# Row maxima of attention scores from sums and differences of two key halves, with two heads stacked on the contraction rows

## The reference

```python
q = (hn @ wq + bq).reshape(b, s, NH, D).transpose(0, 2, 1, 3)
k = (hn @ wk + bk).reshape(b, s, NH, D).transpose(0, 2, 1, 3)
v = (hn @ wv + bv).reshape(b, s, NH, D).transpose(0, 2, 1, 3)
scores = jnp.einsum('bhqd,bhkd->bhqk', q, k) / jnp.sqrt(jnp.float32(D))
attn = jax.nn.softmax(scores, axis=-1)
o = jnp.einsum('bhqk,bhkd->bhqd', attn, v)
```

## Time and profile before

| | |
|---|---|
| median of 3 runs | 1525.85 us (1525.6 to 1525.93) |
| profiled execution: its own time, and the span of its instructions | 1527.39 us, 1525.6 us |
| busy over the span: PE, DVE, ACT, POOL | 1326.6, 1080.8, 705.8, 600.5 us |
| mean granted TensorE clock over the span | 0.936 of 2.4 GHz |
| attention phase | from the start to about 1182 us |
| expert phase | from there to the end |

### The profile page before, as it was taken

One profiled execution on the slowest core, in us unless ns is written; L12 is line 12 of the kernel. 1 busy time (PEld: TensorE's weight loads), 2 busy tenths in 40 slices (PEclk: granted clock), 3 DMA queues, 4 the chain that ended last, 5 costly groups with the idle time before them and its releaser, 6 DMA issues. The chain is left out here.

```text
span 1525.6 us, 24394 instructions
## 1 busy us (share of the span) xinstructions
PE 1326.6 (87%) x6498; PEld 878.6 (58%) x6498; DVE 1080.8 (71%) x5685; ACT 705.8 (46%) x1531; POOL 600.5 (39%) x751
## 2 busy tenths in 40 slices
PE   6756779989998998998899899899897299999996
PEld 2444346455555646555554564554434299998996
DVE  1495998999899899999989989985552622222222
ACT  2323425736654664675575457356454022222221
POOL 5035333334243324424343433341101256766663
PEclk9977889999998999999999899989998599999998
DMA  6201522163061344217125332621721446266551
GB/s 230 74 1 35 109 52 63 69 141 57 22 166 43 64 108 101 64 56 154 34 51 124 78 71 78 125 43 70 147 29 56 138 132 209 71 236 229 182 177 30
DMA packets 91946, 149.42 MB, mean 98 GB/s; under 512 B 34578, under 2 KB 43160, under 8 KB 87736
## 3 DMA queue, kind: packets, MB, share of 16 engines
q1 hardware_dynamic: 73736, 94.97, 26.4%
q0 software_dynamic: 18096, 53.19, 10.8%
HBM read 153.94 MB, written 42.86 MB: 129 GB/s over the span
## 5 line engine op out<-in xcount | busy, mean ns | idle before, releaser
L1079 DVE TENSOR_REDUCE nmax<-fr 128x1 f32<-128x512 f32 x512 | 330.0, 679 | 56.8 <-PE fr L539 56.3
L872 ACT ACTIVATE pt<-fr 128x512 f32<-128x512 f32 x512 | 276.4, 608 | 92.6 <-PE fr L539 89.9
L539 PE MATMUL fr<-ks,qs 128*128 128x512 f32 x512 | 220.9, 486 | 30.6 <-DVE nmax L1079 14.2
L539 PE MATMUL fr<-qs,ks 128*128 128x512 f32 x512 | 204.9, 477 | 20.5 <-DVE nmax L1079 12.8
L1181 POOL TENSOR_TENSOR m<-m,e 128x1024 f32<-128x1024 f32 x32 | 75.8, 2369 | 259.0 <-DVE m L1015 205.2
L539 PEld LDWEIGHTS fr<-qs,ks 128*128 128x128 f32 x512 | 97.3, 200 | 124.7 <-issue 59.9
L539 PEld LDWEIGHTS fr<-ks,qs 128*128 128x128 f32 x512 | 94.6, 197 | 108.1 <-DVE nmax L1079 48.1
L703 PE MATMUL ob<-pt,v 128*32 128x512 f32 x1024 | 139.6, 618 | 0.5 <-ACT pt L872 0.5
L539 PE MATMUL xs<-M,xnT 128*128 128x512 f32 x256 | 124.8, 611 | 1.2 <-ACT xnT L760 1.0
L539 PE MATMUL xt<-VW,pT 128*128 128x256 f32 x512 | 122.5, 394 | 2.7 <-ACT pT L760 1.3
L539 PEld LDWEIGHTS xt<-VW,pT 128*128 128x128 f32 x512 | 99.3, 198 | 19.2 <-ACT hnT L761 4.5
(11 more groups left out here) (188 smaller groups left out, 2613.0 us busy)
## 6 DMA issues: line engine op xcount, KB each, us to landing
parts_d<-parts SPq DMA_DIRECT2D x32, 512.0 KB, 3.5
qs<-parts_d SPq DMA_DIRECT2D x128, 128.0 KB, 4.1
ks<-parts_d SPq DMA_DIRECT2D x128, 128.0 KB, 5.4
xy_d<-xy SPq DMA_DIRECT2D x32, 256.0 KB, 3.6
xyf<-xy_d SPq DMA_DIRECT2D x32, 256.0 KB, 3.2
rows_d<-row SPq DMA_DIRECT2D x32, 256.0 KB, 3.2
xb<-x SPq DMA_DIRECT2D x16, 256.0 KB, 2.9
kbd<-kT_d SPq DMA_DIRECT2D x16, 128.0 KB, 3.3
```

Source lines behind the costliest of these rows:

```text
L539: return pe.matmul(o, l, r, start=first, stop=last)
L872: act.activation(pt[:, t % 2, h, :], fr_bank(b, "st", 16 * g + n)[:, :], ACT.Exp, scale=D ** -0.5)\
L1079: v.tensor_reduce(nmax[:, g % 2, 4 * h + t:4 * h + t + 1], fr_bank(b, "fs", 16 * g + n)[:, :], AX.X, ALU.max, negate=True).then_inc(fr_sig ...
```

## The change

- **Two heads stacked.** `qs` and `ks` hold two heads one above the other, 64 rows each (for every head dimension its four high and low parts), in half as many column blocks. Each matmul of both passes works on 64 rows, rows 0 to 63 or 64 to 127; the two of a pair are issued one after the other, into two banks of `fr`.
- **Sums and differences.** A third projected matrix, "d", is made from k: PE multiplies k's two parts by `unit` and `minus`, so that its first 256 columns hold key s plus key s + 256 and the last 256 their difference. It is split, stored and loaded like q and k, into `kd`. The first pass multiplies by `kd`, so a score tile holds 256 sums and 256 differences.
- **The maximum** of a pair of keys is half of (sum + absolute difference). ACT takes the absolute value of the 256 differences into one of four buffers `apart` (`abs_out`), and DVE, in one `tensor_tensor_reduce` over 256 columns, adds the sums, halves, and takes the row maximum.
- **The subtraction.** `nmax` is now wide (72 columns per query tile), `max_turn` has four transposes per group, `max_out` writes `cB` (72 x 512, negated), and the DMA `max_load` is gone. In the second pass a second matmul of 64 rows per head (`sel` times `cB`) adds minus the maximum into the same bank.
- **Banks.** `xs` becomes three banks, shared in turn by all that used `xs` and `xt`.
- `PERIOD` and all places in `AT` are new; the steps "fs" and "st" now each stand for a pair, "ab" is new, "cl" is gone.

The core of the diff (all entries of `AT`, most semaphores and the replaced names of `xt_...` by `xs_...` are left out):

```diff
-PERIOD = 134.36
+PERIOD = 127.73
...
+NXS, NFR = 3, 4
+XS_TURN = turns("M", "VW", "sc", "pT", "xt", "av", "yt")
+FR_TURN = turns("proj", "v", "ct", "ot", "oT", "wo", "zT", "gt", pairs=("fs", "st"))
...
-STACK = 16 * 9
+STACK = 16 * 12
+NABS = 4
...
+NC = 64 + 2 * NT
 SLOT = (0, 1, 2, 0)
-PROJ = (("q", 0), ("k", 0), ("q", 1), ("k", 1))
+PROJ = (("q", 0), ("k", 0), ("d", 0), ("q", 1), ("k", 1), ("d", 1))
...
+        kd = sa("kd", [P, 2 * NSLOT, S], F32R)
+        unit = sa("unit", [P, P], F32R)
+        minus = sa("minus", [P, P], F32R)
+        apart = sa("apart", [P, NABS, S // 2])
+        sel = sa("sel", [P, 2, P], F32R)
+        pick_rows = sa("pick_rows", [P, 2])
         v32 = sa("v32", [P, NT, NH, VC])
...
+        nmax = sa("nmax", [P, 2, NT, NC])
+        cB = sa("cB", [P, 2, S], F32R)
...
-        xs = [bank(f"xs{n}") for n in range(2)]
-        xt = bank("xt")
+        xs = [bank(f"xs{n}") for n in range(NXS)]
+        xt = xs[2]
...
                     sp.wait_ge(q, 32 * b + 16 + 16 * (g // 2))
 
                 def rows(part):
-                    return parts_d[part, 64 * g:64 * g + 64, :].rearrange("(h d) s -> d h s", d=D)
+                    return parts_d[part, 64 * g:64 * g + 64, :].rearrange("(p x) s -> x p s", p=2)
 
                 for r, part in enumerate((0, 0, 1, 1)):
-                    sp.dma_start(qs[D * r:D * r + D, sl, :].bitcast(F32), rows(part)).then_inc(stack_loaded[slot], 16)
+                    sp.dma_start(qs[r:P:4, sl, :].bitcast(F32), rows(part)).then_inc(stack_loaded[slot], 16)
                 for r, part in enumerate((2, 3, 2, 3)):
-                    sp.dma_start(ks[D * r:D * r + D, sl, :].bitcast(F32), rows(part)).then_inc(stack_loaded[slot], 16)
-                sp.dma_start(qs[4 * D:4 * D + 1, sl, :].bitcast(F32).rearrange("o h (t c) -> o (h t) c", c=P),
-                             zrow[:, :]).then_inc(stack_loaded[slot], 16)
-
-            def max_load(b):
-                for g in range(G):
-                    yield due(b, "cl", g)
-                    sl = slice(4 * SLOT[g], 4 * SLOT[g] + 4)
-                    fr_read(sp, b, "ct", g)
-                    sp.dma_start(qs[4 * D:4 * D + 1, sl, :].bitcast(F32).rearrange("o h (t c) -> o (h t) c", c=P),
-                                 cT[:, :].bitcast(F32)).then_inc(c_loaded, 16)
+                    sp.dma_start(ks[r:P:4, sl, :].bitcast(F32), rows(part)).then_inc(stack_loaded[slot], 16)
+                for r, part in enumerate((4, 5, 4, 5)):
+                    sp.dma_start(kd[r:P:4, sl, :].bitcast(F32), rows(part)).then_inc(stack_loaded[slot], 16)
 
             def xy_load(b):
...
                 for n, (name, mt) in enumerate(PROJ):
                     yield due(b, "proj", n)
                     if n == 0:
-                        xt_read(pe, b, "yt", NT - 1)
+                        xs_read(pe, b, "yt", NT - 1)
                     o = fr_slot(b, "proj", n)
+                    if name == "d":
+                        fr_read(pe, b, "proj", n - 1)
+                        for half, sign in enumerate((unit, minus)):
+                            for j in range(4):
+                                key = slice(S // 2 * (j // 2), S // 2 * (j // 2 + 1))
+                                ins = mm(o[:, S // 2 * half:S // 2 * (half + 1)], (unit if j < 2 else sign)[:, :],
+                                         parts[:, (n - 1) % 3, j % 2, key], j == 0, j == 3)
+                        ins.then_inc(fr_full, 1)
+                        continue
                     for k in range(KT):
...
             def first_pass(b, g):
-                for n in range(16):
-                    t, h = n // 4, n % 4
-                    yield due(b, "fs", 16 * g + n)
+                for n in range(0, 16, 2):
+                    t, pair = n // 4, 2 * SLOT[g] + n % 4 // 2
+                    yield due(b, "fs", 8 * g + n // 2)
                     slot = SLOT[g]
                     if n == 0:
                         pe.wait_ge(stack_loaded[slot], STACK * (b * SLOT.count(slot) + SLOT[:g + 1].count(slot)))
-                    o = fr_slot(b, "fs", 16 * g + n)
-                    mm(o[:, :], qs[:, 4 * slot + h, t * P:(t + 1) * P], ks[:, 4 * slot + h, :]).then_inc(fr_full, 1)
+                    for i in range(2):
+                        half = slice(64 * i, 64 * i + 64)
+                        o = fr_slot(b, "fs", 16 * g + n + i)
+                        mm(o[:, :], qs[half, pair, t * P:(t + 1) * P], kd[half, pair, :]).then_inc(fr_full, 1)
 
             def max_turn(b, g):
                 yield due(b, "ct", g)
                 fr_read(pe, b, "fs", 16 * g + 15)
                 o = fr_slot(b, "ct", g)
-                tr(o[0:4 * NT, 0:P], nmax[:, g % 2, :]).then_inc(fr_full, 1)
+                for t in range(NT):
+                    ins = tr(o[0:NC, t * P:(t + 1) * P], nmax[:, g % 2, t, :])
+                ins.then_inc(fr_full, 1)
 
             def second_pass(b, g):
-                for n in range(16):
-                    t, h = n // 4, n % 4
-                    yield due(b, "st", 16 * g + n)
-                    sl = 4 * SLOT[g] + h
+                for n in range(0, 16, 2):
+                    t, p = n // 4, n % 4 // 2
+                    pair = 2 * SLOT[g] + p
+                    yield due(b, "st", 8 * g + n // 2)
                     if n == 0:
-                        pe.wait_ge(c_loaded, 16 * (G * b + g + 1))
-                    o = fr_slot(b, "st", 16 * g + n)
-                    mm(o[:, :], ks[:, sl, t * P:(t + 1) * P], qs[:, sl, :]).then_inc(fr_full, 1)
+                        fr_read(pe, b, "ct", g)
+                    halves = [slice(64 * i, 64 * i + 64) for i in range(2)]
+                    o = [fr_slot(b, "st", 16 * g + n + i) for i in range(2)]
+                    for i in range(2):
+                        mm(o[i][:, :], ks[halves[i], pair, t * P:(t + 1) * P], qs[halves[i], pair, :], True, False)
+                    for i in range(2):
+                        mm(o[i][:, :], sel[halves[i], p, :], cB[halves[i], g % 2, :], False, True).then_inc(fr_full, 1)
 
...
             def parts_high(b):
                 for n, (name, mt) in enumerate(PROJ):
                     yield due(b, "ph", n)
                     fr_written(act, b, "proj", n)
-                    wait(act, parts_stored[n % 2], 16 * (2 * b + n // 2))
-                    copy(parts[:, n % 2, 0, :], fr_bank(b, "proj", n)[:, :], 1.0, cv("b" + name, mt)).then_inc(part_hi, 1)
+                    wait(act, parts_stored[n % 3], 16 * (2 * b + n // 3))
+                    bias = None if name == "d" else cv("b" + name, mt)
+                    copy(parts[:, n % 3, 0, :], fr_bank(b, "proj", n)[:, :], 1.0, bias).then_inc(part_hi, 1)
 
...
+            def abs_out(b, g):
+                for n in range(16):
+                    yield due(b, "ab", 16 * g + n)
+                    fr_written(act, b, "fs", 16 * g + n)
+                    last = before(b, 16 * g + n, NABS, 16 * G)
+                    if last is not None:
+                        fr_read(act, last[0], "fs", last[1])
+                    act.activation(apart[:, n % NABS, :], fr_bank(b, "fs", 16 * g + n)[:, S // 2:], ACT.Abs).then_inc(abs_ready, 1)
+
             def max_out(b, g):
                 yield due(b, "co", g)
                 fr_written(act, b, "ct", g)
-                wait(act, c_loaded, 16 * (G * b + g))
-                copy(cT[:, :], fr_bank(b, "ct", g)[0:4 * NT, 0:P]).then_inc(fr_signal(b, "ct", g), 1)
+                last = before(b, g, 2, G)
+                if last is not None:
+                    fr_written(act, last[0], "st", 16 * last[1] + 15)
+                copy(cB[0:NC, g % 2, :], fr_bank(b, "ct", g)[0:NC, :], -1.0).then_inc(fr_signal(b, "ct", g), 1)
...
             def parts_low(b):
                 for n, (name, mt) in enumerate(PROJ):
                     yield due(b, "pl", n)
-                    dve.wait_ge(part_hi, 4 * b + n + 1)
-                    v.scalar_tensor_tensor(parts[:, n % 2, 1, :], fr_bank(b, "proj", n)[:, :], cv("b" + name, mt),
-                                           parts[:, n % 2, 0, :].bitcast(F32), ALU.add, ALU.subtract)\
-                     .then_inc(fr_signal(b, "proj", n), 1)
+                    dve.wait_ge(part_hi, 6 * b + n + 1)
+                    o, high, low = fr_bank(b, "proj", n), parts[:, n % 3, 0, :].bitcast(F32), parts[:, n % 3, 1, :]
+                    if name == "d":
+                        ins = v.tensor_tensor(low, o[:, :], high, ALU.subtract)
+                    else:
+                        ins = v.scalar_tensor_tensor(low, o[:, :], cv("b" + name, mt), high, ALU.add, ALU.subtract)
+                    ins.then_inc(fr_signal(b, "proj", n), 1)
 
             def maxima(b, g):
                 for n in range(16):
@@ -1075,9 +1110,11 @@
                     last = before(b, g, 2, G)
                     if n == 0 and last is not None:
                         fr_written(dve, last[0], "ct", last[1])
```

(33 more changed lines are left out.)

151 lines of the change are left out of this document (83 added, 68 removed), and 138 rows, old and new, of the table AT.

## The result

The changed kernel takes 1568.47 us, the median of four runs (1561.55 to 1573.86), against 1525.72 for the kernel before on the same chip: a ratio of 1.028 with a 95% interval of 1.0228 to 1.0333, so 43 us slower. I had predicted 1480 us, with a chance of 0.73 for faster. The profiled execution took 1573.86 us, with a span of 1571.8.

The account below looks back on a forecast made before the run. DVE, 93% busy in the middle gaps, was taken as the bound. DVE at 111.1 plus 12 idle gives gaps of 123.1, 6.6 below 129.7, 46 us over seven: 1525.9 - 46 = 1480 us, range 1415 to 1535.

Parts of the forecast that it names:

- The step that failed: Middle gaps: DVE, 121.2 us busy per batch, is the bound; PE's 106 us, 84% of a gap, isn't.
- A second step: ACT's queue: its work grows from 76.9 to 96.4 us per batch, 76% of a gap, hidden if the order allows.
- DVE, the maxima: First-pass row maxima: 64 new reductions at a step of 0.42 us, 26.9 instead of 38.3 per batch, saving 11.4.
- first rival: DVE's new reduction is slow, 0.66 us a step, so DVE has 126.5 us per batch: 1563 us, chance 0.10.
- ACT: Per batch: absolute values 17.3 us, high parts of "d" 1.0, wider copy into `cB` 1.2; 76.9 becomes 96.4.
- PE: Per batch: passes 5.4 us less, "d" 1.9, wider turn 1.3 and mode changes 4.8 more; 106 becomes 109.
- second rival: Both passes: pairs of 64 rows don't overlap, PE needs 129 us per batch: 1573 us, chance 0.12.
- Idle allowed to grow to 12: Gaps: DVE's idle time was let grow from 8.5 to 12 us, giving a gap of 123.1.
- third rival: Chain PE, ACT, DVE through four banks stalls all three, a gap stays at 126 us: 1517 us, chance 0.15.
- The base of the sum: All seven gaps: each gains the 6.6 us by which 123.1 is below the middle gaps' 129.7, 46 us together.
- Drain, start, expert phase at nothing: Drain and expert phase: 0 us; in the drain a saving and a longer wait were both set at 5 us.
- SP, DMA, ring of banks at nothing: Ten more DMA issues and 3 MB more per batch taken as hidden; three `xs` banks in turn cost nothing.

Follow-up runs that it names:

- run 11: Kernel before with each maximum taken over 328 of the 512 columns, so less DVE work: 1489.43 us, ratio 0.9749.
- run 15: Kernel before without the replacing of found values in nhi, 64 DVE instructions per batch: 1494.08 us, ratio 0.9806.
- run 16: Changed kernel without the replacing of found values in nhi, 10.2 us per batch less on DVE: 1534.25 us, ratio 1.0068 to the kernel before.
- run 7: Changed kernel with the new reduction over 128 columns instead of 256: 1555.29 us, ratio 1.0212 to the kernel before.
- run 10: Kernel before with each second-pass matmul issued twice into the same bank: 1604.26 us, ratio 1.0541.
- run 5: Changed kernel without the 64 subtraction matmuls of `sel` and `cB` per batch: 1543.1 us, ratio 1.0126 to the kernel before.
- run 6: Changed kernel without the absolute values on ACT; the reduction adds a constant tile: 1540.73 us, ratio 1.0119 to the kernel before.
- run 9: Changed kernel without both the subtraction matmuls and the absolute values: 1520.61 us, ratio 0.9996 to the kernel before.
- run 13: Kernel before with 24 more narrow matmuls per batch on 64 rows, adding mode changes: 1560.17 us, ratio 1.0226.
- run 14: Kernel before with 24 more narrow matmuls per batch on all 128 rows, without mode changes: 1533.09 us, ratio 1.0073.
- run 3: Changed kernel keeping only the stacking of two heads, without sums, differences and absolute values, in the new order: 1627.06 us, ratio 1.0672 to the kernel before.
- run 4: Changed kernel keeping only the stacking of two heads, in the order of the kernel before: 1647.01 us, ratio 1.0807 to the kernel before.
- run 12: Changed kernel with ACT's absolute values made from a constant tile and the reduction waiting for PE alone: 1553.15 us, ratio 1.0198 to the kernel before.
- run 1: Kernel before with only the two xs banks and the xt bank made one ring of three: 1523.3 us, ratio 1.0004.
- run 2: Kernel before with the ring of three banks and the changed kernel's order on every queue, computation unchanged: 1600.74 us, ratio 1.0512.
- run 8: Changed kernel with all its work, in the order (`AT` and `PERIOD`) of the kernel before: 1809.77 us, ratio 1.1884 to the kernel before.

## Why the prediction was wrong

What a microsecond of each kind is worth in the time of the whole kernel (all eight batches):

| work | run | us of work | us of time | worth |
|---|---|---|---|---|
| DVE, maxima (before) | 11 | -90 | -38 | 0.42 |
| DVE, picks (before) | 15 | -78 | -30 | 0.38 |
| DVE, picks (after) | 16 | -80 | -32 | 0.40 |
| DVE, maxima (after) | 7 | -52 | -10 | 0.2 |
| PE, second pass (before) | 10 | +118 | +82 | 0.70 |
| PE, subtraction (after) | 5 | -79 | -23 | 0.29 |

PE's -79 is an estimate, 8 x 32 steps of 0.31. A worth is known to 0.1 or so to either side, that of run 7 to 0.2. Work that is added and work that is taken off need not count alike: the 0.70 is of the first kind, all the others are of the second, and no run took work off PE or put work on DVE in the kernel before.

**The step that failed** is "So a microsecond off DVE counts until PE or ACT, or the order, takes over", with its counterpart that PE's 106 us, "84% of a gap", lie hidden behind DVE. I read DVE's 93% busy as one bound that holds all along. Runs 10 and 11 show otherwise in the unchanged kernel: PE, by my steps the idler engine, passes on 0.70 of what is put on it, and DVE only 0.42 of what is taken off. A second step fell with it, that ACT's added work "hides behind DVE if the order lets it": leaving the absolute values out gives 25 us (run 6), and after the change DVE waits for ACT 20 us a batch.

What is shown is this. Of the change's work, subtraction and absolute values cost 23 and 25 us (runs 5 and 6), and without both the kernel is 43 us faster, as fast as the one before (run 9). What DVE lost, 12.6 us a batch or 101 in eight, gives by the worths above 101 x 0.4 = 40 us and not 101.

How the rest adds up is an estimate, and it doesn't close. To the 23 and 25 come 49 mode changes a batch, 8 x 49 x 0.06 = 24 us (runs 13 and 14); less the 40 that is +32. The matmuls of "d" and the wider turn are 3.2 us a batch by my sum, 7 to 18 us at PE's two worths; no run left them out. Against that the pairs save steps: by the steps seen, 13.9 us for 14.7 in the first pass, and 32 x 0.31 = 9.9 for 14.7 in the second without its subtraction, 5.6 a batch, 13 to 31 us. Together some +19 to +26 of the measured +43. And the same prices make the stacking alone some +23 to +37, where runs 3 and 4 measured +102 and +123. So a price found in one kernel and order does not carry over to another, and what the stacking costs through the banks and the order stays open.

Point by point:

- *DVE, the maxima.* Right in kind and somewhat dear: the step is 0.34, not 0.42. DVE's busy time fell by 12.6, not 10.1. The first rival is out. By the Trainium skill ("VectorE: DVE Perf Modes", section "Two Vector instructions with no wait between them") such an operation is two instructions; the trace agrees, and shows that the second, of 0.08, lies beside the next reduction. The Trainium skill's half rate ("Vector Engine (DVE) Microarchitecture Reference", section 7, "Points that are easy to get wrong") is for two sources in SBUF that aren't bf16; here one is in PSUM and it is not seen, 256 columns in 0.34 us, and no run has both in SBUF.
- *ACT.* Work right, 98.4 against 96.4. That it hides behind DVE was wrong: half of the 25 us is ACT's own time (run 12), half the link over a third queue.
- *PE.* Pairs on rows run at once, so the second rival's reason is out, and its time of 1573 us came by another way. Mode changes: 81 counted in the trace, 80 forecast, at 0.09 instead of 0.1. Too cheap were the pairs: 64 steps of 0.31 instead of 0.25 add 3.8, and a first pass of 22 pairs and 19 singles at some 0.34 takes 13.9 instead of 8, 5.9 more, a part of it waiting for banks. So PE asks for about 118, not 109, and if all of it grew with the clock, 0.93 instead of 0.97, for 123 of a gap of 136.7, by estimate. The 106 of before were too low in the same way. I had read the step of 0.23 off four matmuls in a row; of the 220 places in the middle gaps before where one matmul of a pass follows another, 59 have a step under 0.26, 81 one of 0.26 to 0.36, and 80 a longer one.
- *Idle allowed to grow to 12.* It grew to 28 in the middle. My third rival had this mechanism (PE, ACT, DVE through four banks; DVE's waits above show it), but at 1517 us, since it too took PE's work as free.
- *The base of the sum.* I took the 6.6 us of the middle gaps for all seven, whose mean was 127.3 and not 129.7, while the second and third rivals reckon from 127.3. From there a gap of 123.1 gains 29 us and the forecast is 1496. This alone doesn't explain the loss.
- *Drain, start, expert phase at nothing.* The start gained 12.5 us, the drain lost 4.
- *SP, DMA, ring of banks at nothing.* Right for the ring (run 1). Of DVE's longer waits one ends with a transfer, that of `x`: 8.3 us in the four middle gaps, 2.4 before. It comes with the order as well (11.2 in run 2); what it costs wasn't tried.

Why an engine that is idle 21% of the time still counts for 0.4 I can't settle. The queues are coupled through four banks and a written order, and a late instruction on any of them can shift the others; that this is the reason was not shown. Run 8 shows how much such an order alone can cost. That some stretches are DVE's and others PE's, my reason for runs 15 and 16, isn't borne out: the worth is the same at both places, within 0.1. Open too is what the best order for the new work would give, and what the halves would give without the stacks; no run tried either. No version here beats the kernel before with all of its computation in place.

## What to carry to other kernels

Before trading one engine's time for another's in a kernel whose queues are ordered by hand, measure what a microsecond is worth on each: one run that issues a matmul twice and one that reduces fewer columns would have shown 0.70 and 0.42. With these and my own counts the forecast would have been 8 x 10.1 x 0.42 = 34 us gained and 8 x 2.6 x 0.70 = 15 lost, 19 faster instead of 46: nearer, and still of the wrong sign. For the sign the added work on the third engine, 25 us for ACT, had to be priced too; with it the same sum gives 6 slower. A busy share of 93% beside one of 84% doesn't name a bound when both are chained through a few banks. Take the step of an instruction from all its places and not from the best one. Count what makes a split of the array pay (a second bank free at the right moment, few changes of mode), and don't judge new work in an order that was made for the old.

## What the runs showed of the hardware

- The granted clock was at its lower level in stretches behind pauses of PE. Windows of 8 us in after, in the middle of a gap:

```profile
601.00:609.00 8.00, 8.00 (x31) 4.70 (x30) 8.00 (x41) 2.33 (x8) 1.98 (x1) 1.00 0.64 204
609.00:617.00 8.00, 6.26 (x34) 3.04 (x36) 7.25 (x53) 6.51 (x16) 2.30 (x2) 0.93 0.26 77
617.00:625.00 8.00, 7.82 (x52) 2.52 (x44) 6.33 (x71) 5.86 (x13) 1.90 (x1) 0.86 0.09 24
625.00:633.00 8.00, 5.95 (x20) 3.04 (x16) 7.20 (x45) 5.57 (x16) 0.00 (x0) 0.78 0.58 175
633.00:641.00 8.00, 7.48 (x30) 4.28 (x31) 6.97 (x36) 4.94 (x12) 1.39 (x1) 0.58 0.00 0
641.00:649.00 8.00, 8.00 (x60) 3.73 (x59) 7.08 (x59) 6.08 (x12) 2.88 (x2) 1.00 0.01 3
```

  PE is busy 6.3 of 8 us in the second of these and 6.0 in the fourth. A mean of 0.58 in the fifth is a mix of the levels 2.4 and 1.2 GHz, though PE is busy 7.5 us of it, and the clock is full again in the next, which PE fills. Over the middle gaps it was 1.00 in run 11, 0.97 before, 0.93 after and 0.88 in run 8. PE's busy share over a gap doesn't tell it: that was 94% in run 11 at 1.00, and 94% in run 9 at 0.93. Matmuls took longer at the lower level, the first of these at a granted clock of 0.50, the second at 1.00:

```profile
616.65 1.93 PE L713 MATMUL ob<-pt,v 128*32 128x512 f32 x8
...
619.96 1.07 PE L713 MATMUL ob<-pt,v 128*32 128x512 f32 x8
```

  That is part of every price above; what alone would hold the clock up wasn't tried.
- Two fp32r matmuls of 64 rows and 512 columns, on different rows and into different banks, start 0.003 us apart and have records of 0.50 us, as one on all rows has. The next pair starts after 0.23 us at best, most often after 0.30 to 0.36.
- The read of the accumulator behind a combined reduction takes 0.08 us and overlaps the next one.
- A change between 64 rows and 128 costs PE 0.08 to 0.09 us (runs 13 and 14).
